# Expert biases carried by the weight loads and a product in plain fp32, and one attention chunk's output work regrouped, in an attention and mixture-of-experts kernel

## The chip, the cores and the metric

The kernel runs on one core of a Trainium2 chip. The metric is the time of one execution on the device in microseconds. The kernel before takes 384.93 us (median of 3 runs, 384.72 to 385.65).

## The reference

Input x is 2048 tokens of 128 numbers, all fp32. Two residual layers follow each other:

```
x = x + attn(layernorm(x))      # 16 heads of 64, linear attention with cos/sin weights,
                                # causal; (num / den) @ Wo + bo
x = x + ffn(layernorm(x))
ffn: logits = xf @ gate_w                       # 8 experts
     top_w, top_idx = top_k(logits, 2); top_w = softmax(top_w)
     h = gelu(xf @ w1[e] + b1[e])               # 128 -> 512
     y = h @ w2[e] + b2[e]                      # 512 -> 128
     out = sum over the two chosen e of y * top_w
```

The biases b1 and b2 are not zero here.

## The kernel before, in words

Tokens are cut into 16 chunks of 128, and four chunks make a unit; there are four units (NS). A unit has a front (projections of q, k and v as products of fp32 numbers split into a high and a low part, on the tensor engine) and then attention over its 16 groups of four heads, taken two at a time as pairs p. Each engine has its program written out by hand in one order; semaphores hold one engine for another. In a unit of the first three, the tensor engine does at the end of a pair: p = 3 and 5, `turn_out` of chunks 0 and 1 (eight transposes, L1238); p = 6, `project` of chunks 0 and 1 (32 instructions of L1247) and `turn_x` (the next unit's input, L1092); p = 7, `turn_out` of chunk 2; p = 8, `project` of chunk 2. Chunk 3 is turned and projected in the next front. The vector engine adds the projections to x (`residual`, L806).

While unit i is in its front and attention, the second layernorm, the gate and the routing of unit i-1 run beside it. The gate (`gate`) is `split3`: three products with split inputs for each chunk. The vector engine picks the two best experts, and GpSimd scatters every token's row, 128 numbers, its id and its weight, to its place in a DRAM buffer ybuf (L480), where every expert has its stretch. The output bias b2 is added per token: the vector engine builds a 128 x 8 matrix of weights for each chunk (`combine`), the tensor engine turns it (`turn_comb`, L1267), the scalar engine copies it, the tensor engine multiplies it by b2 (`biases`, L1273) and the vector engine adds the result (`open_sum`, L948). This is done for units 0 and 1 in the fronts of units 2 and 3, and for units 2 and 3 among the expert blocks.

The expert stage is 39 blocks (NB) of 128 rows of one expert. A small table, made in two parts (17 blocks, then 22), holds each block's expert and place. `block_table` makes it with products, four of which (L1302) fetch b1 for each block. SyncE's queue loads a block in `load_block`:

```
if b >= YR: sp.wait_ge(z_out[(b - YR) % ZR], ...)
at = sp.value_load(tab[0:1, 1, b:b + 1], ...)                  # L379
sp.dma_start(yb[b % YR][:], ybuf[bass.ds(at, TB), :])          # L380, the rows
if b >= WR: sp.wait_ge(h_ps, 2 * (b - WR) + 2)
sp.dma_start(w1b[b % WR][:], w1[bass.ds(at // PITCH, 1), ...]) # L383, the weights
```

YR = 10 row buffers, ZR = 8 result buffers and WR = 6 weight buffers go round. All of w2 stays in SBUF. A `step(b)` of the tensor engine is: transpose block b+2's rows (L1376), `hidden(b+1)` (eight instructions of L1389), `down(b)` (eight of L1404, into one PSUM bank). `down(b)` waits until the vector engine has taken block b-1's result. `weighed` (L1020) takes it: result times the row's weight, from PSUM into z. GpSimd scatters z to DRAM (L518); the results come back at the end (zin) and are added to x (L1027, L1029) and stored.

Of the kernel before, what the change touches and what calls it, by code (L numbers as in the profile page):

```python
# [28 lines left out]
P = 128  # L29
# [7 lines left out]
SC = 4  # L37
# [21 lines left out]
COMB_AT, BIAS_AT, BIAS_AFTER = 7, 9, 4  # L59
# [3 lines left out]
STATS_AFTER, NORM_AFTER, NORMED_AFTER, YLOW_AFTER, BEST_AFTER = 1, 2, 3, 5, 6  # L63
# [28 lines left out]
def moe_block(nc, x, Wq, bq, Wk, bk, Wv, bv, Wo, bo, gate_w, w1, b1, w2, b2,  # L92
              c_rot, c_pair, c_ident, c_small, c_tri, c_ids, out, ybuf, zbuf):
    with ExitStack() as ctx:
# [13 lines left out]
        gate_hi = sb("gate_hi", [P, E], F32R)  # L108
        gate_lo = sb("gate_lo", [P, E], F32R)
        brows = sb("brows", [2 * NP, P])  # L110
        bcols = sb("bcols", [P, 2 * NP])
        b1q = sb("b1q", [QC, F])
        bv_all = sb("bv_all", [P, HD])
        bo_all = sb("bo_all", [P, D])
        b2_sb = sb("b2_sb", [P, D])
# [25 lines left out]
        oT = sb("oT", [P, 2, NP, P])  # L141
# [6 lines left out]
        yT_hi = sb("yT_hi", [P, ST], F32R)  # L148
        yT_lo = sb("yT_lo", [P, ST], F32R)
# [9 lines left out]
        hotw = sb("hotw", [P, 2, SC, E])  # L159
# [11 lines left out]
        b1t = sb("b1t", [P, FB, NB])  # L171
        tab = sb("tab", [1, 2, NB], I32)
        comb = sb("comb", [P, SC, E])
        combT = sb("combT", [P, SC, P])
        yb = [sb(f"yb{k}", [P, ROW]) for k in range(3)]
        w1b = [sb(f"w1b{k}", [P, F]) for k in range(2)]
# [21 lines left out]
        w1b += [sb(f"w1b{k}", [P, F]) for k in range(2, WR)]  # L198
# [12 lines left out]
        b1_in = sem("b1_in")  # L211
# [58 lines left out]
        yThi_ok = sem("yThi_ok")  # L270
        yTlo_ok = sem("yTlo_ok")
# [9 lines left out]
        hotw_ok = sem("hotw_ok")  # L281
        any_ok = sem("any_ok")
        comb_ok = sem("comb_ok")
        cT_ps = sem("cT_ps")
        cT_ok = sem("cT_ok")
        b2_ps = sem("b2_ps")
        acc0_ok = sem("acc0_ok")
# [32 lines left out]
        def _(sp):  # L320
# [14 lines left out]
            sp.wait_ge(memsets, 2)  # L335
            sp.dma_start(b2_sb[0:E, :], b2).then_inc(c_in, 16)
# [15 lines left out]
            sp.wait_ge(memsets, 6)  # L352
# [10 lines left out]
            for e in range(E):  # L363
                sp.dma_start(b1q[e * QC // E:(e + 1) * QC // E, :], b1[e:e + 1, :].broadcast_to([QC // E, F])
                             ).then_inc(b1_in, 16)
# [47 lines left out]
        def _(pool):  # L413
            pool.memset(neg_half[:], -0.5).then_inc(memsets, 1)
            pool.memset(b2_sb[:], 0.0).then_inc(memsets, 1)
            pool.memset(combT[:], 0.0).then_inc(memsets, 1)
# [11 lines left out]
            pool.wait_ge(memsets, 5)  # L428
# [61 lines left out]
            def attention(i):  # L490
# [3 lines left out]
                for c in range(SC):  # L494
# [4 lines left out]
                    if c == 0:  # L499
                        if i == 0:  # L500
                            pool.wait_ge(c_in, 16 * 4)
# [37 lines left out]
        def _(act):  # L539
# [13 lines left out]
            act.wait_ge(row_in, 16 * 3)  # L553
            act.activation(gate_hi[:], gate_sb[:], ACT.Copy).then_inc(whi_ok, 1)
            act.wait_ge(bT_ok, 1)

            def turn_out(i, c):

                for half in range(2):
                    act.wait_ge(oT_ps, i * 2 * SC + 2 * c + half + 1)  # L560
                    act.activation(oT[:, c % 2, half * 4:half * 4 + 4, :],
                                   ps[:, 6 + half, :].rearrange("p (a b) -> p a b", b=P), ACT.Copy
                                   ).then_inc(oT_ok, 1)

            def front(i, tail):
# [5 lines left out]
                for j in range(QK_JOBS):  # L571
# [11 lines left out]
                    if i >= 2 and j == COMB_AT:  # L583
                        comb_turned(i - 2)
                keys(K_JOBS - 1)

            def y_turned(u, bank):
                n = len(UNITS[u][1]) * P
                act.wait_ge(yT_ps, u + 1)
                act.activation(yT_hi[:, 0:n], ps[:, bank, 0:n], ACT.Copy).then_inc(yThi_ok, 1)  # L590
# [9 lines left out]

            def comb_turned(i):
                act.wait_ge(cT_ps, i + 1)
                if i >= 1:
                    act.wait_ge(b2_ps, i)
                act.wait_ge(memsets, 4)
                act.activation(combT[0:E, :, :], ps[0:E, 7, :].rearrange("p (a b) -> p a b", b=P), ACT.Copy).then_inc(cT_ok, 1)
# [38 lines left out]
            def hidden(b):  # L645
# [7 lines left out]
                for f in range(FB):  # L653
                    if f % 2 == 0:
                        act.wait_ge(h_ps, b * 2 + f // 2 + 1)
                    act.activation(hT[:, b % 2, f, :], ps[:, b % 2 * 2 + f // 2, f % 2 * P:f % 2 * P + P], ACT.Gelu,  # L656
                                   bias=b1t[:, f, b:b + 1]).then_inc(h_ok, 1)
# [13 lines left out]
            for b in range(5, NB):  # L671
                hidden(b)
                if b == 10:
                    comb_turned(NS - 2)
                if b == 12:
                    comb_turned(NS - 1)
# [10 lines left out]
        def _(dve):  # L687
# [54 lines left out]
            def front(i, tail):  # L742
                angles(i)
                ones_columns(i)
                for m in range(V_JOBS):
                    if m == V_JOBS - 1:
                        if not tail:
                            dve.wait_ge(c_in, 16 * 4)
# [4 lines left out]
                    if not tail and m == 0:  # L753
                        low_half(0, 3)
                        dve.wait_ge(whi_ok, 4)
                        dve.tensor_tensor(gate_lo[:], gate_sb[:], f32(gate_hi[:]), ALU.subtract).then_inc(wlo_ok, 1)
# [6 lines left out]
                    if i >= 2 and m == BIAS_AFTER:  # L763
                        open_sum(i - 2)
                    if tail and m == YLOW_AFTER:
                        y_low(i - 1)
# [72 lines left out]
            def y_low(u, bank=6):  # L839
                n = len(UNITS[u][1]) * P  # L840
                dve.wait_ge(yThi_ok, u + 1)
                dve.tensor_tensor(yT_lo[:, 0:n], ps[:, bank, 0:n], f32(yT_hi[:, 0:n]), ALU.subtract).then_inc(yTlo_ok, 1)

# [35 lines left out]

            def combine(i):  # L880

                dve.wait_ge(wts_ok, i + 1 if i < NS - 1 else NU)
                if i >= 1:
                    dve.wait_ge(cT_ps, i)
# [625 lines left out]
```

## Time and profile before

| what | value |
|---|---|
| median of the runs shown | 384.93 us |
| the profiled execution: time | 386.15 us |
| the profiled execution: first to last instruction (span) | 384.3 us |
| tensor engine busy (of the span) | 353.2 us (92%) |
| vector, scalar, GpSimd busy | 61%, 41%, 34% |
| mean granted clock of the tensor engine | 0.98 |
| share of the chain that ended last: tensor engine, DMA, vector engine | 79%, 6%, 6% |

The profiled execution's own time is 1.85 us above its span and 1.22 us above the median. SPq is SyncE's instruction queue; its DMA rows are the time of the issue alone, and the transfer runs after it.

### The profile page before, as it was taken

The numbers are of one execution on the slowest core, as the hardware profiler recorded it, in microseconds if no ns is written. First come the engines' busy times: TensorE is split into PE (matmuls) and PEld (weight loads), VectorE is DVE, ScalarE is ACT, GpSimd is POOL, SyncE is SP. The second block draws the span as 40 slices with busy tenths as digits, with TensorE's granted clock in tenths as the row PEclk, the third lists the DMA queues.
The fourth block names the chain that finished last, engine by engine and source line by source line (L and its number), as shares of the span: only waits on it lengthen the run. The fifth ranks groups of instructions, "written<-read, shape, count | busy, mean of one in ns | idle before, by whom it ended". The sixth has DMA issues, their size and how long they took to land.

```text
span 384.3 us, 10812 instructions
## 1 busy us (share of the span) xinstructions
PE 353.2 (92%) x4167; PEld 320.9 (83%) x4167; DVE 236.3 (61%) x677; ACT 158.9 (41%) x374; POOL 130.4 (34%) x132
## 2 busy tenths in 40 slices
PE   0899999999999999999999999999999999999910
PEld 0677999988899988889999888999799999999910
DVE  4689864668886466797646678875646433222205
ACT  2575232267323136732322673122245455666600
POOL 5013241103058310304840130352326755555520
PEclk9999999999999999999999999999999999999975
DMA  7741332334001000000100001700463557877439
GB/s 250 197 185 63 147 143 107 131 124 159 2 31 33 25 9 3 0 2 26 40 25 9 2 0 31 206 25 20 115 172 109 163 142 211 231 200 205 124 83 244
DMA packets 32753, 38.35 MB, mean 100 GB/s; under 512 B 4115, under 2 KB 25008, under 8 KB 31680
## 3 DMA queue, kind: packets, MB, share of 16 engines
q1 hardware_dynamic: 27232, 31.62, 27.2%
q0 software_dynamic: 2272, 4.46, 3.3%
q10 hardware_dynamic: 3200, 1.58, 1.6%
q8 instruction: 34, 0.56, 0.6%
q14 instruction: 15, 0.12, 0.1%
HBM read 22.63 MB, written 15.47 MB: 99 GB/s over the span
## 4 chain that ended last, share of the span: by engine, by line
PE 79%; DMA 6%; DVE 6%; issue 3%; POOL 3%; SPq 1%; ACTq 0%; ACT 0%; POOLq 0%; DVEq 0%
PE ps L1211 8%; PE ps L1173 8%; PE ps L1404 7%; PE ps L1389 7%; PE ps L1190 7%; PE ps L1218 7%; PE ps L1247 7%; PE ps L1085 6%; PE ps L1087 6%; PE ps L1086 6%; PE ps L1238 4%; PE ps L1130 3%; DMA zin<-zbuf 2%; DMA yb<-ybuf 2%; POOL ybuf L480 2%
## 5 line engine op out<-in xcount | busy, mean ns | idle before, releaser
L615 ACT ACTIVATE os<-ps 128x260 f32<-128x260 f32 x64 | 24.8, 388 | 100.5 <-PE ps L1218 100.5
L656 ACT ACTIVATE hT<-ps,b1t 128x128 f32<-128x128 f32 x156 | 44.5, 368 | 34.8 <-PE ps L1389 34.0
L480 POOL DMA_INDIRECT ybuf<-yr,slot x32 | 31.7, 991 | 72.8 <-issue 37.4
L438 POOL TENSOR_TENSOR on<-tcs,rden 128x1024 f32<-128x1024 f32 x16 | 30.4, 1901 | 64.8 <-DVE rden L801 64.8
L518 POOL DMA_INDIRECT zbuf<-z,yb x39 | 37.9, 972 | 30.3 <-DVE z L1020 26.3
L788 DVE TENSOR_TENSOR state<-ps,state 128x260 f32<-128x260 f32 x64 | 27.4, 428 | 31.4 <-ACT os L615 29.1
L778 DVE TENSOR_TENSOR am<-ps,pair 128x1024 f32<-128x1024 f32 x32 | 38.7, 1210 | 9.9 <-issue 6.6
L1020 DVE TENSOR_SCALAR z<-ps,yb 128x128 f32<-128x128 f32 x39 | 13.7, 351 | 47.2 <-PE ps L1404 47.2
L1404 PE MATMUL ps<-w_sb,hT 128*128 x312 | 41.7, 277 | 0.8 <-DVE z L1020 0.8
L1211 PE MATMUL ps<-vcs,am 128*64 128x65 f32 x1024 | 42.2, 225 | 0.0
L1389 PE MATMUL ps<-xb,w1b 128*128 128x128 f32 x312 | 41.2, 276 | 0.0
L1211 PEld LDWEIGHTS ps<-vcs,am 128*64 128x64 f32 x1024 | 36.8, 137 | 3.9
L1218 PE MATMUL ps<-vcs,kn 128*64 128x130 f32 x512 | 39.5, 275 | 0.0
L1404 PEld LDWEIGHTS ps<-w_sb,hT 128*128 128x128 f32 x312 | 38.0, 192 | 1.4 <-issue 1.2
L1389 PEld LDWEIGHTS ps<-xb,w1b 128*128 128x128 f32 x312 | 38.1, 193 | 0.0
L1173 PE MATMUL ps<-qT,kT 64*128 64x128 f32 x512 | 37.2, 285 | 0.9 <-DVE am L778 0.9
L1173 PEld LDWEIGHTS ps<-qT,kT 64*128 64x128 f32 x512 | 31.1, 188 | 6.7 <-issue 6.2
L733 DVE TENSOR_TENSOR os<-ps,bv_all 128x512 f32<-128x512 f32 x32 | 22.1, 690 | 18.2 <-PE ps L1087 18.2
L1190 PE MATMUL ps<-state,qT 64*128 64x130 f32 x480 | 33.2, 277 | 0.0
L1247 PE MATMUL ps<-wo_sb,oT 128*128 128x128 f32 x256 | 31.6, 279 | 0.0
L737 DVE TENSOR_SCALAR vcs<-os,cs 128x512 f32<-128x512 f32 x64 | 30.9, 525 | 1.1
L1247 PEld LDWEIGHTS ps<-wo_sb,oT 128*128 128x128 f32 x256 | 29.8, 192 | 1.7 <-issue 1.4
(136 smaller groups left out, 619.6 us busy)
## 6 DMA issues: line engine op xcount, KB each, us to landing
w1b<-in_L_ffn_w SPq DMA_DIRECT2D x39, 256.0 KB, 3.1
ybuf<-blank SPq DMA_DIRECT2D x8, 1152.0 KB, 4.6
yb<-ybuf SPq DMA_DIRECT2D x39, 72.0 KB, 3.0
w_sb<-in_L_ffn_w SPq DMA_DIRECT2D x8, 256.0 KB, 4.6
x_sb<-in_L_attn_x SPq DMA_DIRECT2D x4, 256.0 KB, 5.2
pair<-c_pair SPq DMA_DIRECT2D x16, 64.0 KB, 2.0
zin<-zbuf SPq DMA_DIRECT2D x4, 256.0 KB, 5.6
zin<-zbuf ACTq DMA_DIRECT2D x4, 256.0 KB, 6.1
```

Source lines behind the costliest of these rows:

```text
L480: pool.indirect_dma_start(ybuf, bass.IndirectOffsetOnAxis(ap=slot[:, k, c:c + 1], axis=0), yr[:, k, c, :], None).then_inc(y_out[u], 16)
L518: pool.indirect_dma_start(zbuf, bass.IndirectOffsetOnAxis(ap=yb[b % YR][:, D:D + 1].bitcast(U32), axis=0), z[:, b % ZR, :], None, bounds_c ...
L656: act.activation(hT[:, b % 2, f, :], ps[:, b % 2 * 2 + f // 2, f % 2 * P:f % 2 * P + P], ACT.Gelu, bias=b1t[:, f, b:b + 1]).then_inc(h_ok, 1)
L737: last = dve.tensor_scalar(vcs[:, m // 2, (m % 2) * 8:(m % 2) * 8 + 8, s, 0:DH], vb[:, m % 2, :].rearrange("p (h d) -> p h d", d=DH), cs4[ ...
L778: dve.tensor_tensor(am[:, p % 2, :, :, :], ps[:, 0:2, :].rearrange("p r (q t) -> p r q t", t=P), pair[:, c, None, None, :].broadcast_to([P ...
L1173: last = mm(ps[:, r, b * P:(b + 1) * P], kT[rows, of, c * P:(c + 1) * P], qT[rows, of, c * P:(c + 1) * P], start=True, stop=True)
L1190: mm(ps[:, 2 + 2 * (n % 2) + r, 0:2 * CS].rearrange("p (s b v) -> p b s v", s=2, b=2)[:, q, :, :], qT[rows, 2 * g + q, c * P:(c + 1) * P], ...
L1211: mm(ps[t:t + 64, 2 + 2 * (n % 2) + r, q * VW:q * VW + VW], am[:, n // 2 % 2, r, (2 * g + q) % (PH // 2), t:t + 64], vcs[:, c, g * GH + 2 ...
L1218: last = mm(ps[64 * r:64 * r + 64, 2 + 2 * (n % 2) + q, 2 * CS:3 * CS], kn[:, c, (2 * g + q) * P + r * DH:(2 * g + q) * P + (r + 1) * DH], ...
L1247: last = mm(ps[:, 7, at:at + D], oT[:, c % 2, pr, :], wo_sb[:, pr, :], start=(pr == 0), stop=(pr == NP - 1))
L1389: last = mm(ps[:, b % 2 * 2 + f // 2, f % 2 * P:f % 2 * P + P], w1b[b % WR][:, f * P:(f + 1) * P], xb[:, b % XR, :], start=True, stop=True ...
L1404: last = mm(ps[:, 4, 0:D], hT[:, b % 2, f, :], w, start=(f == 0), stop=(f == FB - 1))
```

## The change

Six edits are made at once.

1. b1 is laid behind w1 on the host, so that a row of an expert's weights has 516 numbers in place of 512; the gelu takes its bias from there. The b1 loads, the four products of each table and the copy of b1t go away.
2. b2 comes by a third DMA in every `load_block`, one row of 128 numbers spread to 128 partitions, into six buffers b2b. `weighed` is two instructions: result plus b2b into zs, then zs times the weight into z. The matrix, its transposes, the bias products and `open_sum` go away for all four units.
3. `down` waits for zs (zs_ok), and the weight load of block b waits for zs of block b-6, in place of the hidden products of block b-6.
4. The gate is one plain fp32 product per chunk in place of three split ones; the vector engine's y_low goes away.
5. In the first three units, pair 6 has no projections; pair 7 has `third_chunk`: half of chunk 2's transposes, the projections of chunks 0 and 1, the other half; both halves use PSUM bank 6. Chunk 2 is projected in the next front after block 1. oT has three buffers.
6. The residual of chunks 0 and 1 stands after pair 7's groups on the vector engine.

```diff
+    columns = b.reshape(E, FB, P).transpose(0, 2, 1)
+    return np.ascontiguousarray(np.concatenate([w, columns], axis=2))
...
                 if b >= WR:
-                    sp.wait_ge(h_ps, 2 * (b - WR) + 2)
+                    sp.wait_ge(zs_ok, b - WR + 1)
                 sp.dma_start(w1b[b % WR][:], w1[bass.ds(at // PITCH, 1), :, :].rearrange("e p n -> p (e n)")
+                             ).then_inc(w1_in[b % WR], 16)
+                sp.dma_start(b2b[:, b % WR, :], b2[bass.ds(at // PITCH, 1), :].broadcast_to([P, D])
                              ).then_inc(w1_in[b % WR], 16)
...
                 dve.wait_ge(z_ps, b + 1)
+                dve.tensor_tensor(zs[:, b % 2, :], ps[:, 4, 0:D], b2b[:, b % WR, :], ALU.add).then_inc(zs_ok, 1)
                 if b >= ZR:
                     dve.wait_ge(z_out[b % ZR], 16 * (b // ZR))
-                dve.tensor_scalar(z[:, b % ZR, :], ps[:, 4, 0:D], yb[b % YR][:, D + 1:D + 2], None, ALU.mult
+                dve.wait_ge(zs_ok, b + 1)
+                dve.tensor_scalar(z[:, b % ZR, :], zs[:, b % 2, :], yb[b % YR][:, D + 1:D + 2], None, ALU.mult
...
-                if b == 10:
-                    open_sum(NS - 2)
-                    combine(NS - 1)
-                if b == 12:
-                    open_sum(NS - 1)
...
-                    if i >= 2 and j == COMB_AT:
-                        pe.wait_ge(x2_ok, i * SC)
-                        turn_comb(i - 2)
-                    if i >= 2 and j == BIAS_AT:
-                        biases(i - 2)
...
+            def third_chunk(i):
+                pe.wait_ge(on_ok, i * SC + 3)
+                turn_half(i, 2, 0, 6)
+                pe.wait_ge(oT_ok, i * 2 * SC + 4)
+                project(i, 0)
+                project(i, 1)
+                pe.wait_ge(oT_ok, i * 2 * SC + 5)
+                turn_half(i, 2, 1, 6)
...
-                    last = split3(ps[:, bank, c * E:(c + 1) * E], (yT_hi, yT_lo), (gate_hi, gate_lo),
-                                  lambda t: t[:, c * P:(c + 1) * P], lambda t: t[:])
+                    last = mm(ps[:, bank, c * E:(c + 1) * E], yT[:, c * P:(c + 1) * P], gate_sb[:], start=True, stop=True,
+                              skip_group_check=True)
...
-                for f in range(FB):
-                    mm(ps[:, bank, 352 + f * n:352 + (f + 1) * n], b1q[:, f * P:(f + 1) * P], match[:, 0:n],
-                       start=True, stop=True, skip_group_check=True)
...
-                    pe.wait_ge(z_ok, b)
+                    pe.wait_ge(zs_ok, b)
```

SyncE's queue, one block of the expert stage. Before (L379 reads the table, yb are the rows, w1b the weights):

```order
L379 TENSOR_LOAD tab
L379 ISA x2
L380 ISA
L380 DMA yb<-ybuf 128x144
L383 ISA
L383 DMA w1b<-in_L_ffn_w 128x512
```

The same block in the changed kernel, where b2b is the spread row of b2:

```order
L359 TENSOR_LOAD tab
L359 ISA x2
L360 ISA
L360 DMA yb<-ybuf 128x144
L363 ISA
L363 DMA w1b<-in_L_ffn_w 128x516
L365 ISA
L365 DMA b2b<-in_L_ffn_b 128x128
```

A register instruction and a DMA are added to each of the 39 blocks, between a block's weights and the next block's rows.

The tensor engine at the end of the first unit's attention, before, from the last groups of pair 6 (L1211, L1218: products of one group; L1173: scores; L1190: products with the state):

```order
L1218 MATMUL ps<-vcs,kn 64x130 x4
L1247 MATMUL ps<-wo_sb,oT 128x128 x16
L1092 MATMUL ps<-ident,xh 128x128 x4
L1173 MATMUL ps<-qT,kT 128x128 x8
L1190 MATMUL ps<-state,qT 128x2x65 x8
L1211 MATMUL ps<-vcs,am 64x65 x8
L1218 MATMUL ps<-vcs,kn 64x130 x4
L1211 MATMUL ps<-vcs,am 64x65 x8
L1218 MATMUL ps<-vcs,kn 64x130 x4
L1238 MATMUL ps<-ident,on 128x128 x8
L1190 MATMUL ps<-state,qT 128x2x65 x8
```

In the changed kernel, the same place:

```order
L1142 MATMUL ps<-vcs,kn 64x130 x4
L1021 MATMUL ps<-ident,xh 128x128 x4
L1097 MATMUL ps<-qT,kT 128x128 x8
L1114 MATMUL ps<-state,qT 128x2x65 x8
L1135 MATMUL ps<-vcs,am 64x65 x8
L1142 MATMUL ps<-vcs,kn 64x130 x4
L1135 MATMUL ps<-vcs,am 64x65 x8
L1142 MATMUL ps<-vcs,kn 64x130 x4
L1158 MATMUL ps<-ident,on 128x128 x4
L1185 MATMUL ps<-wo_sb,oT 128x128 x16
L1158 MATMUL ps<-ident,on 128x128 x4
L1114 MATMUL ps<-state,qT 128x2x65 x8
```

The 16 products stand between two halves of the transposes; `turn_x` stays where it is, behind pair 6.

The vector engine in the expert stage, before (xb is a turned block of rows):

```order
L1013 COPY xb<-ps 128x128
L1020 TENSOR_SCALAR z<-ps,yb 128x128
L1013 COPY xb<-ps 128x128
L1020 TENSOR_SCALAR z<-ps,yb 128x128
L1013 COPY xb<-ps 128x128
```

and in the changed kernel:

```order
L948 COPY xb<-ps 128x128
L953 TENSOR_TENSOR zs<-ps,b2b 128x128
L957 TENSOR_SCALAR z<-zs,yb 128x128
L948 COPY xb<-ps 128x128
L953 TENSOR_TENSOR zs<-ps,b2b 128x128
L957 TENSOR_SCALAR z<-zs,yb 128x128
```

Each block's result passes through two instructions, and only the first reads PSUM.

## Rows read from the trace of the kernel before

**Rows 1.** The page, busy time of each engine

```profile
PE 353.2 (92%) x4167; PEld 320.9 (83%) x4167; DVE 236.3 (61%) x677; ACT 158.9 (41%) x374; POOL 130.4 (34%) x132
```

**Rows 2.** Waits of the tensor engine: us, times, longest

```profile
PE ps L1313 <- DMA yb<-ybuf: 0.6, 1, 0.6
PE ps L1376 <- DMA yb<-ybuf: 0.3, 1, 0.3
```

**Rows 3.** Tensor engine in order of time, third front: start us, us

```profile
153.33 0.60 PE L1267 MATMUL ps<-ident,comb 128*8 128x128 f32 x4
153.76 0.60 PE L1130 MATMUL ps<-ident,kT 128*128 128x128 f32 x4
...
164.96 0.24 PE L1085 MATMUL ps<-gate_hi,yT_hi 128*128 128x8 f32 x1
165.06 0.25 PE L1086 MATMUL ps<-gate_lo,yT_hi 128*128 128x8 f32 x1
```

**Rows 4.** Chain of waits, expert stage, the bias product: start us, us

```profile
317.29 0.89 PE ps L1273 x8
```

**Rows 5.** Tensor engine, last unit, first block table

```profile
263.93 1.07 PE L1302 MATMUL ps<-match,b1q 128*128 128x17 f32 x8
264.93 0.20 PE L1304 MATMUL ps<-match,small 128*1 128x17 f32 x2
```

**Rows 6.** Tensor engine, end of the first unit, next front

```profile
61.61 3.84 PE L1247 MATMUL ps<-wo_sb,oT 128*128 128x128 f32 x32
65.28 0.60 PE L1092 MATMUL ps<-ident,xh 128*128 128x128 f32 x4
...
73.87 2.05 PE L1247 MATMUL ps<-wo_sb,oT 128*128 128x128 f32 x16
75.68 0.48 PE L1085 MATMUL ps<-xT_hi,W 128*128 128x512 f32 x1
```

**Rows 7.** Load queue (SPq) in order of time, expert stage

```profile
274.13 0.34 SPq L380 DMA_DIRECT2D yb<-ybuf  x1
...
316.56 0.34 SPq L380 DMA_DIRECT2D yb<-ybuf  x1
...
318.36 0.33 SPq L380 DMA_DIRECT2D yb<-ybuf  x1
318.92 0.33 SPq L383 DMA_DIRECT2D w1b<-in_L_ffn_w  x1
320.03 0.33 SPq L380 DMA_DIRECT2D yb<-ybuf  x1
...
336.00 1.33 SPq L383 DMA_DIRECT2D w1b<-in_L_ffn_w  x1
...
356.22 0.33 SPq L380 DMA_DIRECT2D yb<-ybuf  x1
```

**Rows 8.** Waits of the load queue, 308 to 360 us

```profile
SPq L379 <- DMA zbuf<-z,yb: 6.6, 3, 4.0
```

**Rows 9.** Page, DMA issues: KB each, median us to landing

```profile
yb<-ybuf SPq DMA_DIRECT2D x39, 72.0 KB, 3.0
```

**Rows 10.** Chain of waits, expert blocks and the end

```profile
321.98 0.11 PE ps L1376
...
361.79 0.11 PE ps L1376
...
365.51 0.36 DVE z L1020
```

**Rows 11.** Windows: busy us per engine (instructions), clock, DMA share, GB/s

```profile
104.00:108.00 4.00, 4.00 (x84) 3.70 (x82) 3.34 (x12) 0.87 (x3) 0.00 (x0) 1.00 0.06 16
344.00:350.00 6.00, 6.00 (x56) 6.00 (x55) 1.64 (x6) 3.73 (x15) 3.22 (x4) 1.00 0.77 221
```

**Rows 12.** Vector engine beside GpSimd, start of the second front

```profile
76.17 1.63 DVE L1001 COPY cnt<-small 128x8 f32<-128x8 f32 x1
```

**Rows 13.** GpSimd in the same stretch

```profile
75.87 1.91 POOL L438 TENSOR_TENSOR on<-tcs,rden 128x1024 f32<-128x1024 f32 x1 [10.36 <-DVE rden L801]
```

More of the change, by code:

```diff
@@ L170, in moe_block @@
         match = sb("match", [QC, NB])
-        b1t = sb("b1t", [P, FB, NB])
         tab = sb("tab", [1, 2, NB], I32)
-        comb = sb("comb", [P, SC, E])
-        combT = sb("combT", [P, SC, P])
         yb = [sb(f"yb{k}", [P, ROW]) for k in range(3)]
-        w1b = [sb(f"w1b{k}", [P, F]) for k in range(2)]
+        w1b = [sb(f"w1b{k}", [P, F + FB]) for k in range(2)]
+        b2b = sb("b2b", [P, WR, D])
+        zs = sb("zs", [P, 2, D])
         xb = sb("xb", [P, XR, P])
@@ L197, in moe_block @@
         w2_sb = sb("w2_sb", [P, E, F])
-        w1b += [sb(f"w1b{k}", [P, F]) for k in range(2, WR)]
+        w1b += [sb(f"w1b{k}", [P, F + FB]) for k in range(2, WR)]
         zin = sb("zin", [P, 2, NC, D])
@@ L656, in hidden @@
                     act.activation(hT[:, b % 2, f, :], ps[:, b % 2 * 2 + f // 2, f % 2 * P:f % 2 * P + P], ACT.Gelu,
[L657 removed]
+                                   bias=w1b[b % WR][:, F + f:F + f + 1]).then_inc(h_ok, 1)
             y_turned(NS - 1, 7)
@@ L964, in attention @@
                             residual(i, p // 2 - 2)
-                        elif p == 7:
-                            residual(i, 0, 2)
                     if tail and p == 1:
@@ L986, in attention @@
                         x_low(i + 1)
+                    if p == PAIRS - 1 and i + 1 < NS:
+                        residual(i, 0, 2)
             norm1_stats(0)
@@ L1142, in front @@
                         turn_out(i - 1, SC - 1)
+                    if tail and j == 1:
+                        project(i - 1, SC - 2)
                     if tail and j == WO_AT:
@@ L1229, in outputs, with turn_half @@
                     within(i, n, opening)
+            def turn_half(i, c, half, bank):
+                for q in range(4):
+                    pr = half * 4 + q
+                    last = pe.transpose(ps[:, bank, q * P:(q + 1) * P],
+                                        on[:, c % 2, 2 * pr:2 * pr + 2, :].rearrange("p h d -> p (h d)"), ident[:])
+                last.then_inc(oT_ps, 1)
             def turn_out(i, c):
                 pe.wait_ge(on_ok, i * SC + c + 1)
-                for half in range(2):
-                    if half == 1 and c >= (1 if i == NS - 1 else 2):
-                        pe.wait_ge(x2_ok, i * SC + c)
-                    for q in range(4):
-                        pr = half * 4 + q
-                        last = pe.transpose(ps[:, 6 + half, q * P:(q + 1) * P],
-                                            on[:, c % 2, 2 * pr:2 * pr + 2, :].rearrange("p h d -> p (h d)"),
-                                            ident[:])
-                    last.then_inc(oT_ps, 1)
+                turn_half(i, c, 0, 6)
+                if c >= (1 if i == NS - 1 else 3):
+                    pe.wait_ge(x2_ok, i * SC + c)
+                turn_half(i, c, 1, 7)
+            def third_chunk(i):
[6 more added lines that the diff above has]
+                turn_half(i, 2, 1, 6)
             def project(i, c):
@@ L1245, in project @@
                 at = D if c == 1 and i < NS - 1 else 0
+                if c == 2 and i < NS - 1:
+                    pe.wait_ge(x2_ok, i * SC + 2)
                 for pr in range(NP):
-                    last = mm(ps[:, 7, at:at + D], oT[:, c % 2, pr, :], wo_sb[:, pr, :], start=(pr == 0), stop=(pr == NP - 1))
+                    last = mm(ps[:, 7, at:at + D], oT[:, c % 3, pr, :], wo_sb[:, pr, :], start=(pr == 0), stop=(pr == NP - 1))
                 last.then_inc(wo_ps, 1)
@@ L1336, in attention @@
                             pe.wait_ge(xTlo_ok, i + 2)
-                        turn_out(i, p // 2 - 1)
+                        if p == PAIRS - 1 and i + 1 < NS:
+                            third_chunk(i)
+                        else:
+                            turn_out(i, p // 2 - 1)
                     if p % 2 == 0 and p >= 4:
@@ L1440, in _ @@
             step(9)
-            turn_comb(NS - 2)
-            step(10)
-            biases(NS - 2)
-            step(11)
-            pe.wait_ge(acc0_ok, NS - 1)
-            turn_comb(NS - 1)
-            step(12)
-            biases(NS - 1)
-            for b in range(13, NB):
+            for b in range(10, NB):
                 step(b)
 _INS = ["L0_attn_x", "L0_attn_Wq", "L0_attn_bq", "L0_attn_Wk", "L0_attn_bk", "L0_attn_Wv", "L0_attn_bv",
-        "L0_attn_Wo", "L0_attn_bo", "L0_ffn_gate_w", "L0_ffn_w1", "L0_ffn_b1", "L0_ffn_w2", "L0_ffn_b2"]
+        "L0_attn_Wo", "L0_attn_bo", "L0_ffn_gate_w", "L0_ffn_w1", "L0_ffn_w2", "L0_ffn_b2"]
 def shape_constants():
```

119 lines of the change are left out of this document (21 added, 98 removed).

## The prediction

> **What bounds the kernel now.** I read the page first: the tensor engine is busy 92% of the span, the others far less [rows 1]. Its waits are the second view, and they are nearly nothing once it has started: 0.6 us for the rows of expert block 1 and 0.3 us for a block's rows later on [rows 2]. So instructions taken off this engine shorten the kernel one for one, as long as nothing that it waits for is late. The third view is therefore the one that an engine's busy share does not show: the load queue, which issues each expert block's DMAs. In it the reader is to see the rhythm, not the waits. With no wait in between, a block's rows are issued at 318.36 and the next block's at 320.03, 1.66 us later, of which the second DMA with its register work is 318.92 - 318.36 = 0.56 us [rows 7]. The tensor engine takes one block in (361.79 - 321.98) / 21 = 1.896 us [rows 10]. The queue is thus 88% full in this stage before anything is added, and with its long issues (one of 1.33 us is shown) it needs (356.22 - 318.36) / 21 = 1.80 us a block [rows 7], 95% of the tensor engine's time.
>
> **The change part by part.** Times are of the profiled execution, 386.15 us with a span of 384.3; its 1.85 us outside the span I leave as they are. It lies 1.22 us above the median of the runs, 384.93, and a difference worked out in it is added to the median.
>
> *Bias products in the fronts.* In the fronts of units 2 and 3 go four transposes, 153.76 - 153.33 = 0.43 us [rows 3], and eight product instructions, 0.89 us [rows 4]. The tensor engine is full there, so 2 x 1.32 = 2.6 us come off.
>
> *Gate.* A unit's gate is twelve instructions, 0.10 to 0.11 us from start to start [rows 3]. A plain fp32 product of 128 x 128 weights runs as two instructions, as the eight of L1302 for four products show, at 1.00 / 8 = 0.125 us or less each [rows 5]. So four chunks take eight: 12 x 0.11 - 8 x 0.11 = 0.44 us less, by the dearer row 0.3. Three fronts: 1.3 us (0.9 to 1.3). The two gates of the last unit give 0.2 each, where the engine meets later waits; I count them as nothing.
>
> *Block tables.* The first loses eight instructions, 264.93 - 263.93 = 1.0 us in the last unit's attention [rows 5]. The second's are among the expert blocks, treated below.
>
> *Third chunk.* The same transposes and products are issued as before, in another place. What two stops cost is in two rows: 32 product instructions behind an attention group take 65.28 - 61.61 = 3.67 us, 0.115 each; sixteen take 75.68 - 73.87 = 1.81 us, 0.113 each [rows 6]. Against 0.111 inside a run [rows 4], entering from a group costs 0.1 us or less. And pair 6 keeps a stop, since the input's transposes stay there, as the order shows. I take 0 (from -0.3 for three units to +0.6, should chunk 2's rows or the residual arrive late). The residual of chunk 2 now holds the vector engine until the next front's second block. What is queued behind it is the copy of the angles and the values, for which the tensor engine waits at the next value product. That costs nothing, because the vector engine loses this time already: its first copy there took 1.63 us [rows 12], while GpSimd multiplied from 75.87 to 77.78 [rows 13], and now it starts when GpSimd is done. The Trainium skill, page SBUF — State Buffer, section Who interferes with whom, states that a vector instruction in its two-port mode and a GpSimd instruction shut each other out; the trace agrees in this copy.
>
> Before the expert stage that makes -(2.6 + 1.3 + 1.0) = -4.9 us.
>
> *First rows.* Block 1's rows were issued at 274.13 [rows 7] and the tensor engine already waited for them [rows 2]. A third DMA of block 0 now stands ahead, 0.56 us: +0.6.
>
> *Load queue.* The spread row of b2 adds the same pair to each block that the weights have, a register instruction and a DMA. Its price has bounds: 0 if the issue were hidden, 0.33 us for the bare issue, 0.56 with the register work and the gaps [rows 7]. I take 0.56, since the rows of one block stand end to end in this queue. A block then needs 1.66 + 0.56 = 2.22 us against 1.896 on the tensor engine: the queue becomes the bound. There is no store of loaded blocks to live on, because rows for blocks 10 to 16 wait for results scattered to DRAM (6.6 us of waits) [rows 8]. Block 16's rows are issued at 316.56; I take 315.8 in the changed kernel, as the second table and its b1 products are 1 us shorter ahead of those results. From there are 22 blocks to the last: 22 x 2.22 = 48.8 us. The long issues come on top: before, 356.22 - 316.56 - 22 x 1.66 = 3.1 us in 22 blocks [rows 7]. I keep 3.1 (1.5 if they go by the queue's load, 4.7 by the number of DMAs). The last block's rows are issued at 315.8 + 48.8 + 3.1 = 367.7 us. They land 3.0 us later [rows 9], at 370.7, where the tensor engine turned them at 361.79 before [rows 10]: +8.9 us. All the work that the change takes off the tensor engine among the expert blocks (bias products of two units, the second b1 products, the small gates, about 4 us) is lost in the waits for rows.
>
> The later release of weight buffers (zs of block b-6) costs nothing: when a step starts as its rows land, the end of step b-6 lies some 3.6 us ahead of the issue for block b. The DMA engines have room: a load of 64 KB in 512 byte rows occupied them for 0.06 x 4 = 0.24 us, and the share of 0.77 at 1.8 us a block [rows 11] becomes (1.39 + 0.24) / 2.3 = 0.71.
>
> *Tail.* The last result passes two instructions. The one of before took 0.36 us [rows 10]; I take +0.3 (0.2 to 0.4, and 1 us if GpSimd's scatter holds the second, which reads SBUF alone).
>
> Sum: -4.9 + 0.6 + 8.9 + 0.3 = +4.9 us. The long issues and block 16's start together move it by -2.2 and +2.4. I forecast 384.93 + 4.9 = 389.8 us; the case's own range is 387.6 to 392.2.
>
> The rule that speaks against this: the Trainium skill, page DMA: Bandwidth & Descriptors, section Issuing engines are not separate DMA queues, says that the sequencer's time to start a DMA is usually small beside the DMA itself. The issue is 0.33 us against 3.0 to landing, so the trace agrees for one DMA; but the landings overlap and the issues do not. By the rule the third load would be free, which is the first rival.
>
> **The rivals.**
>
> *The queue keeps up (not slower).* The place is the load queue, and it decides at a price of the third DMA under 1.896 - 1.80 = 0.1 us a block. For it: 95% was enough before, and the bytes are few. Against it: the issues stand end to end without waits. The time: -4.9 before the stage, +0.6, +0.3; among the blocks the queue's start after the scatters holds the engine, so that only the last bias product (0.9 us) is gained: -4.9 us, 380.0 us.
>
> *A thin third DMA.* Should it cost the bare issue, 0.33 us, and the long issues be 1.5 us, the last rows are issued at 315.8 + 22 x 1.99 + 1.5 = 361.1 and land at 364.1, +2.3 us: in all -4.9 + 0.6 + 2.3 + 0.3 = -1.7 to, with the long issues kept, -0.1 us. 384.0 us stands for it.
>
> *The queue and the DMA engines together.* If loads land later because 128 more packets a block share the engines with the scatters, result waits come back on the queue. At 2.5 us a block, 0.28 more than the queue's own pace, it is 22 x 0.28 = 6 us more: 395.8 us. The share of 0.77 speaks for it, the 0.24 us against it.
>
> *The regrouping fails in attention.* Three units in which pair 7 waits a microsecond for the normalised chunk: +3 us, 392.8 us. Against it: pairs 3 and 5 have the same distance from their groups to the transposes, and pair 7 has the input's transposes ahead besides.
>
> **How the numbers follow.** Forecast 0.73; queue keeps up 0.09; thin third DMA 0.08; both together 0.05; attention 0.05. The measurement tells about 0.3% from no change, 1.2 us. Faster by more than that (below 383.8): the first rival and part of the second, 0.12. Within: the rest of the second and the forecast's lowest edge, 0.06. Slower: 0.82. The range 384.0 to 393.2 us leaves the first rival and most of the third outside, with some of the forecast's upper edge, about 0.2.
>
> **What would show it.** In the changed profile the load queue should issue rows every 2.2 us from about block 14 on with hardly a wait, and the tensor engine should wait for yb in most of the last 24 blocks, some 0.4 us each, its busy share in that stage near 80%. The start of the expert stage should lie about 4.9 us earlier than before, and the tensor engine should have no new wait at pair 7 and none in the fronts. The forecast is wrong if the tensor engine's blocks still follow each other at 1.9 us, or if rows are issued earlier than the engine needs them; then the price of the third DMA was the failed step.

## The result and the profile after

| | median | runs | profiled execution | its span |
|---|---|---|---|---|
| before | 384.93 us | 384.72 to 385.65 | 386.15 us | 384.3 us |
| changed | 392.67 us | 391.14 to 393.69 | 391.79 us | 390.0 us |

The ratio is 1.0201, 95% interval 1.0164 to 1.0238: slower by 2%, or 7.7 us, where 389.8 us was forecast (range 384.0 to 393.2; the case's own range, 387.6 to 392.2, is missed by 0.5 us). A fourth execution of the kernel before took 914.58 us and is left out.

The page's first line answers to [rows 1]: the tensor engine has 4.5 us less to do, and yet the span grew by 5.7.

```profile
PE 348.7 (89%) x4087; PEld 314.0 (81%) x4087; DVE 235.3 (60%) x696; ACT 156.9 (40%) x369; POOL 129.9 (33%) x130
```

What it waits for, answering to [rows 2] (us, times, longest): the rows of the expert blocks, 9.3 us where it was 0.3. L1298 is the turning of a block's rows, L1235 that of blocks 0 and 1. The 0.7 us of L1158 is the last chunk's, at 278.92 (0.4 before); at pair 7 and in the fronts there is no new wait.

```profile
PE ps L1298 <- DMA yb<-ybuf: 9.3, 13, 1.4
PE ps L1235 <- DMA yb<-ybuf: 1.0, 1, 1.0
PE ps L1326 <- DVE zs L953: 0.7, 2, 0.5
PE ps L1158 <- POOL on L418: 0.7, 1, 0.7
```

The load queue in order of time (start, us), answering to [rows 7]. Nothing is waited for between these rows. The first two DMAs of a block stand 0.56 us apart as before, the third 0.52 behind the second, and the next block's rows 1.10 behind that: 2.18 us in place of 1.66. The later rows are a long issue and the rows of block 16 and of the last block.

```profile
301.68 1.25 SPq L365 DMA_DIRECT2D b2b<-in_L_ffn_b  x1
...
312.42 0.33 SPq L360 DMA_DIRECT2D yb<-ybuf  x1
...
335.68 0.33 SPq L360 DMA_DIRECT2D yb<-ybuf  x1
336.24 0.33 SPq L363 DMA_DIRECT2D w1b<-in_L_ffn_w  x1
336.76 0.33 SPq L365 DMA_DIRECT2D b2b<-in_L_ffn_b  x1
337.86 0.33 SPq L360 DMA_DIRECT2D yb<-ybuf  x1
...
363.57 0.33 SPq L360 DMA_DIRECT2D yb<-ybuf  x1
```

Its waits between 280 and 370 us, answering to [rows 8]. The last ends with block 13's rows, at 305.67; from there the queue only issues. The 3.3 us are block 6's weights, held until block 0's zs (edit 3). The queue then still waits 2.4 us for block 0's results before block 10's rows, so this wait costs nothing, as the prediction had it.

```profile
SPq L359 <- DMA zbuf<-z,yb: 4.4, 2, 2.4
SPq L363 <- DVE zs L953: 3.3, 1, 3.3
```

The chain that ended last, answering to [rows 10]. Before, it ran through the tensor engine's blocks one after the other; now rows from DRAM stand in it, and the last block's are issued at 363.57 and turned as they land:

```profile
342.37 3.90 DMA yb<-ybuf
346.64 0.90 PE ps L1311 x8
...
356.55 1.38 SPq L363
363.57 3.13 DMA yb<-ybuf
366.71 0.04 issue
366.75 0.33 PE ps L1298
...
370.74 0.30 DVE zs L953
...
372.76 0.49 DVE z L957
...
374.01 2.11 DMA zbuf<-z,yb
```

Windows of the changed kernel, as in [rows 11]. The engine is idle 4.4, 5.0 and 2.4 us in the three (the last is part of the first), at full clock, with the DMA engines at 0.75 to 0.81:

```profile
330.00:368.00 38.00, 33.59 (x282) 32.07 (x282) 13.29 (x49) 18.62 (x66) 15.52 (x16) 1.00 0.75 195
300.00:330.00 30.00, 25.01 (x203) 23.19 (x202) 9.79 (x36) 13.69 (x48) 15.56 (x17) 1.00 0.81 201
330.00:350.00 20.00, 17.64 (x150) 16.93 (x150) 6.79 (x25) 9.95 (x36) 7.76 (x8) 1.00 0.78 205
```

Ahead of the blocks all went as the change says. The third front's gate (answering to [rows 3]) and block 0 and 1's rows at the end of the attention:

```profile
162.83 0.95 PE L1198 MATMUL ps<-gate_sb,yT 128*128 128x8 f32 x8
163.64 0.41 PE L1059 MATMUL ps<-ident,kT 128*128 128x128 f32 x2
...
270.08 0.33 PE L1235 MATMUL ps<-ident,yb 128*128 128x128 f32 x1 [0.25 <-ACT oT L539]
271.42 0.33 PE L1235 MATMUL ps<-ident,yb 128*128 128x128 f32 x1 [1.01 <-DMA yb<-ybuf]
```

The same two, and the last block's, before:

```profile
275.47 0.33 PE L1313 MATMUL ps<-ident,yb 128*128 128x128 f32 x1 [0.25 <-ACT oT L561]
276.37 0.33 PE L1313 MATMUL ps<-ident,yb 128*128 128x128 f32 x1 [0.57 <-DMA yb<-ybuf]
...
361.62 0.27 PE L1376 MATMUL ps<-ident,yb 128*128 128x128 f32 x1
```

So the changed kernel is 5.4 us ahead at block 0, 5.0 at block 1, and 5.1 behind at the last block: 10.1 us are lost among the blocks.

### The profile page after: what moved, and what is told of

Same layout as the page of the kernel before. It is cut to its first block, busy times and chain, and to the rows that moved or that the text cites. A ratio compares the mean times of both kernels' runs of the same rounds, so it can differ in the third digit from the quotient of the medians.

```text
span 390.0 us, 10763 instructions
## 1 busy us (share of the span) xinstructions
PE 348.7 (89%) x4087; PEld 314.0 (81%) x4087; DVE 235.3 (60%) x696; ACT 156.9 (40%) x369; POOL 129.9 (33%) x130
## 4 chain that ended last, share of the span: by engine, by line
PE 69%; DMA 8%; SPq 7%; DVE 7%; issue 5%; POOL 2%; ACT 0%; ACTq 0%; POOLq 0%; DVEq 0%
PE ps L1097 8%; PE ps L1135 8%; PE ps L1114 7%; PE ps L1142 7%; PE ps L1185 6%; PE ps L1014 6%; PE ps L1015 5%; PE ps L1016 5%; PE ps L1326 4%; PE ps L1158 4%; PE ps L1311 3%; DMA yb<-ybuf 3%; PE ps L1059 3%; SPq L359 2%; SPq L363 2%
## 5 line engine op out<-in xcount | busy, mean ns | idle before, releaser
L625 ACT ACTIVATE hT<-ps,w1b 128x128 f32<-128x128 f32 x156 | 44.5, 368 | 47.3 <-PE ps L1311 44.7
L1326 PE MATMUL ps<-w_sb,hT 128*128 x312 | 42.8, 281 | 0.7 <-DVE zs L953 0.7
L953 DVE TENSOR_TENSOR zs<-ps,b2b 128x128 f32<-128x128 f32 x39 | 11.4, 291 | 45.0 <-PE ps L1326 43.7
L702 DVE TENSOR_SCALAR vcs<-os,cs 128x512 f32<-128x512 f32 x64 | 32.6, 552 | 1.1
L1114 PEld LDWEIGHTS ps<-state,qT 64*128 64x128 f32 x480 | 30.2, 188 | 0.8 <-issue 0.7
```

The costliest lines, as they stand in the source:

```text
L702: last = dve.tensor_scalar(vcs[:, m // 2, (m % 2) * 8:(m % 2) * 8 + 8, s, 0:DH], vb[:, m % 2, :].rearrange("p (h d) -> p h d", d=DH), cs4[ ...
L1114: mm(ps[:, 2 + 2 * (n % 2) + r, 0:2 * CS].rearrange("p (s b v) -> p b s v", s=2, b=2)[:, q, :, :], qT[rows, 2 * g + q, c * P:(c + 1) * P], ...
L1326: last = mm(ps[:, 4, 0:D], hT[:, b % 2, f, :], w, start=(f == 0), stop=(f == FB - 1))
```

## The experiments

The theory: the load queue's own issue of a third DMA, about half a microsecond, makes it slower than the tensor engine. The rivals: the extra bytes, or the kind of load (one row spread to 128 partitions); the new arithmetic and waits; the regrouping in attention. Three sets of kernels shared a chip and the kernel before each: its median was 385.15 us beside the first four, 384.96 beside the next four, 385.16 beside the last three.

### The same bytes in two DMAs

b2 is laid behind w1 and b1 on the host, already spread, so that a row has 644 numbers.

```diff
-    return np.ascontiguousarray(np.concatenate([w, columns], axis=2))
+    rows = np.broadcast_to(b2[:, None, :], (E, P, D))
+    return np.ascontiguousarray(np.concatenate([w, columns, rows], axis=2))
...
-                sp.dma_start(b2b[:, b % WR, :], b2[bass.ds(at // PITCH, 1), :].broadcast_to([P, D])
-                             ).then_inc(w1_in[b % WR], 16)
```

> The changed kernel with b2's row laid behind w1 and b1 on the host (a row of 644 numbers), so that a block is two DMAs again; the bytes are those of the changed kernel. Theory (the third issue on the load queue is the price): the queue returns to 1.66 us a block, the tensor engine's waits for yb fall from 9.3 us to about 1, and the time is 379.5 us, 378 to 382. Rival (the 64 KB more a block on the DMA engines are the price): the bytes stay, so the waits stay and the time is at least 388 us. Rival (the second instruction of weighed and the later release of the weight buffers are the price): both stay too, 388 us or more.

Measured: 384.3 us (382.03 to 385.23, 10 runs), ratio 0.9968, interval 0.9947 to 0.9989. Against the changed kernel 8.4 us are back, from the same arithmetic and the same bytes; but not the 379.5 expected (378 to 382). Where the rest is, its tensor engine shows (waits, then windows of 2 us):

```profile
PE ps L1295 <- DMA yb<-ybuf: 2.9, 3, 1.4
...
PE ps L1232 <- DMA yb<-ybuf: 1.8, 1, 1.8
```

```profile
270.00:272.00 2.00, 0.57 (x3) 0.35 (x3) 0.14 (x1) 0.00 (x0) 0.00 (x0) 0.91 0.63 207
272.00:274.00 2.00, 2.00 (x17) 1.81 (x16) 0.28 (x1) 0.38 (x1) 0.00 (x0) 0.50 0.80 214
274.00:276.00 2.00, 2.00 (x44) 1.87 (x44) 0.00 (x0) 0.28 (x1) 0.00 (x0) 0.74 0.87 238
```

It waited 1.8 us for block 1's rows, in part since the issue of block 0's weights, ahead of them on the queue, took 1.12 us:

```profile
266.38 1.12 SPq L362 DMA_DIRECT2D w1b<-in_L_ffn_w  x1
268.29 0.33 SPq L359 DMA_DIRECT2D yb<-ybuf  x1
```

and then ran 3 us (272 to 275) at a granted clock of 0.50, the lower of its two levels (1.2 GHz).

### The same bytes in three DMAs

The row of 644 numbers is loaded in two pieces, of 516 and 128 numbers.

```diff
-                sp.dma_start(w1b[b % WR][:], w1[bass.ds(at // PITCH, 1), :, :]...
+                sp.dma_start(w1b[b % WR][:, 0:F + FB], w1[bass.ds(at // PITCH, 1), :, 0:F + FB]...
+                             ).then_inc(w1_in[b % WR], 16)
+                sp.dma_start(w1b[b % WR][:, F + FB:F + FB + D], w1[bass.ds(at // PITCH, 1), :, F + FB:F + FB + D]...
```

> The kernel of e1_merged with its weight load cut in two DMAs, 516 numbers a row and then 128, same bytes, same buffers. Theory (issue): a block's rows every 2.2 us again, 391 to 394 us, as the changed kernel. Rival (what cost was reading one row of b2 128 times): the source is 128 different rows here, so the time stays near e1_merged. Rival (bytes): no difference between e1_merged and this one.

Measured: 390.96 us (389.79 to 393.03, 6 runs), ratio 1.0152, interval 1.0127 to 1.0177; the expectation said 391 to 394. Its queue has the changed kernel's rhythm, 2.18 us from rows to rows, and its tensor engine the same wait:

```profile
337.65 0.33 SPq L359 DMA_DIRECT2D yb<-ybuf  x1
338.21 0.33 SPq L362 DMA_DIRECT2D w1b<-in_L_ffn_w  x1
338.73 0.33 SPq L364 DMA_DIRECT2D w1b<-in_L_ffn_w  x1
339.83 0.33 SPq L359 DMA_DIRECT2D yb<-ybuf  x1
```

```profile
PE ps L1298 <- DMA yb<-ybuf: 10.1, 12, 1.3
```

Of this pair only the number of DMAs differs (and with it that of their packets, at nearly the same busy share of the DMA engines, 29.2% against 29.0%), and 6.7 us lie between them. So the bytes are not what costs them. The spread source could be worth no more than the 1.7 us from here to the changed kernel, and the runs of the two overlap.

### The third DMA alone, in the kernel before

For blocks 8 to 38 it loads b2's row of the block's expert, spread to 128 partitions, into a free buffer; nothing reads it, but the tensor engine waits until it has landed.

```diff
+                if b >= 8:
+                    sp.dma_start(zin[:, 0, b % WR, :], b2[bass.ds(at // PITCH, 1), :].broadcast_to([P, D])
+                                 ).then_inc(d3_in[b % WR], 16)
...
+                if b >= 8:
+                    pe.wait_ge(d3_in[b % WR], 16 * ((b - 8) // WR + 1))
```

> The kernel before with nothing changed but a third DMA on the load queue for blocks 8 to 38: b2's row spread over 128 partitions into memory that nobody reads. Theory (issue): 31 blocks at 2.2 us from block 14 on; the last rows are issued near 368 us in place of 356.2, and the time is 393.5 us, 391.5 to 396. Rival (the delay comes from what the vector engine does with b2, or from the release of the weight buffers): neither is here, so 385 to 386 us.

Measured: 397.15 us (395.73 to 398.7), ratio 1.0312, interval 1.0285 to 1.0338: 12.0 us for a DMA whose data nobody uses (10.3 by the spans of the profiled executions), above the 391.5 to 396 expected. The last rows go out near the expected 368 us, but they are turned at 371.79, 10.2 us later than before, where the expectation adds 8.6 in all, and 2.8 us of the profiled execution lie outside its span in place of 1.85. Its rows are issued at 316.45 (block 16) and 368.74 (the last), 2.377 us a block, and the tensor engine waits:

```profile
PE ps L1380 <- DMA yb<-ybuf: 7.1, 7, 1.7
```

### The changed kernel without the regrouping

The two stops, the residual and the chunk's projections are put back as they were (edits 5 and 6 undone).

```diff
-                        if p == PAIRS - 1 and i + 1 < NS:
-                            third_chunk(i)
-                        else:
-                            turn_out(i, p // 2 - 1)
+                        turn_out(i, p // 2 - 1)
```

> The changed kernel with the regrouping of chunk 2 undone (pair 6 projects chunks 0 and 1 again, pair 8 chunk 2), biases and gate as changed. Theory (the regrouping is worth 0): the same as the changed kernel within 0.6 us, and the first rows of the expert stage turned at 270.1 to 270.7 us. Rival (the regrouping is what saved the 0.5 us more than forecast before the expert stage): the first rows turned at 270.6 us or later and the time up to 1.5 us longer. Rival (it costs): shorter than the changed kernel by over 1 us.

Measured: 392.9 us (391.47 to 395.71), ratio 1.0217, interval 1.0185 to 1.0249, against 392.67 with it: no difference that these runs, 2.5 and 4.2 us wide, can tell. Its first rows are turned at 269.50, earlier than the 270.1 to 270.7 expected; but the profiles with the regrouping have 269.34 to 270.37, so this does not decide either. Whether the queue hides something is asked again below.

### Block 1's rows ahead of the first weights

Blocks 0 and 1 are loaded as rows, rows, weights, weights, in three kernels: the changed one, the merged row, the kernel before.

```diff
-            load_block(0)
-            load_block(1)
+            for b in range(2):
+                ats.append(sp.value_load(tab[0:1, 1, b:b + 1], min_val=0, max_val=PLACES))
+                sp.dma_start(yb[b][:], ybuf[bass.ds(ats[b], TB), :]).then_inc(yb_in[b], 16)
+            for b in range(2):
+                sp.dma_start(w1b[b][:], w1[bass.ds(ats[b] // PITCH, 1), :, :].rearrange("e p n -> p (e n)")
...
```

> The changed kernel with the rows of blocks 0 and 1 issued before the weights and bias rows of either. Nothing else is moved. Theory (besides the third issue, the wait for block 1's rows, 1.0 us in the profile of the changed kernel, lets the granted clock of the tensor engine fall in some executions, which is why its runs lie between 391.1 and 393.7 us): the wait goes, the runs come together within 1 us, and the median is 390.8 us, 390 to 391.6. The long stretch after block 13 is bound by the load queue as before and gives back part of the gain. Rival (the spread comes from the long issues of the load queue): the median is the changed kernel's, 392 to 393.5, with the same spread.

Measured: 391.3 us (388.9 to 392.36, 6 runs), ratio 1.0153, interval 1.0124 to 1.0182. The median is as expected, 1.4 us under the changed kernel's; but the runs did not come together within 1 us, they lie 3.5 apart. The wait for block 1 is gone, and 8.4 us of waits for rows stay.

> The kernel of e1_merged (two DMAs a block) with the rows of blocks 0 and 1 issued first. In the profile of e1_merged the tensor engine waited 1.8 us for block 1's rows, and the granted clock was 0.50 from 272 to 274 us. Theory (that wait and the clock that fell behind it kept e1_merged from 379.5 us): 381 us, 380 to 382.3, no granted clock under 1.00 between 268 and 290 us. Rival (the clock falls for another reason, or the time was lost at blocks 13 to 15): 383.5 to 384.5 us.

Measured: 379.76 us (379.36 to 380.25, 5 runs), ratio 0.9864, interval 0.9845 to 0.9883. It is 4.5 us under the merged row alone (3.5 by the profiled executions) and just under the expected 380 to 382.3, though the wait removed was 1.8 us. The merged row's ten runs have mean granted clocks from 0.970 to 0.978, these five from 0.977 to 0.982. The clock stays up in the same stretch:

```profile
270.00:272.00 2.00, 2.00 (x36) 1.71 (x38) 0.43 (x1) 0.38 (x1) 0.00 (x0) 1.00 0.89 255
272.00:274.00 2.00, 2.00 (x41) 1.82 (x38) 0.88 (x3) 0.78 (x2) 0.00 (x0) 1.00 0.81 243
```

> The kernel before with the rows of blocks 0 and 1 issued first. It waited 0.6 us for block 1's rows, with the clock at 1.00. Theory: 0.3 to 0.8 us less than before, 384.6 us. Rival (an order of loads that only helps where the clock falls): no difference within 0.3 us.

Measured: 384.92 us (384.04 to 385.71, 12 runs), ratio 0.9992, interval 0.9979 to 1.0006: no difference, as the rival said, where 0.3 to 0.8 us were expected. The order of the first loads gave much, 4.5 us, in the one kernel where the profile shows the clock fall behind the wait.

### Twelve row buffers in place of ten

```diff
-YR, ZR, WR, XR = 10, 8, 6, 4
+YR, ZR, WR, XR = 12, 8, 6, 4
```

On the merged row with block 1's rows first:

> The kernel of e6 with 12 row buffers in place of 10, so that block b's rows wait for the results of block b-12 and not b-10. Theory (in e1_merged the last loss of time is that blocks 13 to 15 wait for results scattered late, 2.9 us of waits in all): 2 us less than e6, 379 us, 378 to 380.5. Rival (the queue's own 1.66 us a block leaves too small a lead, or the waits move to another block): within 0.7 us of e6.

Measured: 376.9 us (375.93 to 378.43, 6 runs), ratio 0.9792, interval 0.9766 to 0.9818. This is 2.9 us under ten buffers, where 2 were expected (378 to 380.5). It is the best of all versions, 2.1% faster than the kernel before. Its tensor engine hardly waits for rows, is full where the changed kernel's was not, and the queue waits again:

```profile
PE ps L1300 <- DMA yb<-ybuf: 0.4, 1, 0.4
```

```profile
300.00:330.00 30.00, 29.65 (x263) 29.28 (x262) 11.76 (x45) 17.71 (x63) 18.80 (x20) 1.00 0.85 244
330.00:350.00 20.00, 20.00 (x182) 20.00 (x181) 8.55 (x33) 11.72 (x42) 10.34 (x11) 1.00 0.86 241
```

```profile
SPq L362 <- DVE zs L955: 11.2, 13, 6.3
```

The same on the kernel before (also with rows first), as a control (the text says 8 row buffers where it means ten):

> The kernel before, with the rows of block 1 asked for ahead of the first weights and 12 row buffers in place of 8; still two DMAs a block. Theory: this kernel's stretch of the blocks was bound by the tensor engine, with about 1 us of waits for rows in it, so the buffers can give back only that: 384.5 us, between 383.5 and 385.5. Rival: the buffers alone are what the merged row with 12 buffers gained over the merged row with 8 (2.9 us), whatever the arithmetic: 382.

Measured: 384.55 us (383.87 to 384.89, 12 runs), ratio 0.9976, interval 0.9963 to 0.999. Two DMAs a block and a full tensor engine: the buffers give 0.4 us. The other 7.6 us of the version above (384.55 - 376.9) come from the change with its merged row.

On that version, with the regrouping undone:

> The merged row with block 1's rows first and 12 row buffers, and the projections of the chunks regrouped back as they were before the change. Theory: the regrouping is worth nothing: within 0.5 us of the same kernel with it (376.9). Rival: with the queue no longer the bound, what the regrouping gives or takes ahead of the blocks shows: 1 us or more to either side.

Measured: 377.2 us (376.18 to 377.93), ratio 0.9785, interval 0.9766 to 0.9805, against 376.9 with it. With hardly a wait for rows to hide it, the regrouping still gives and takes nothing that can be told: runs of one kernel lie 1.8 and 2.5 us apart here.

On the changed kernel with its three DMAs (and rows first):

> The changed kernel, three DMAs a block, with block 1's rows first and 12 row buffers. Theory: the load queue issues at its own 2.18 us a block, and buffers help it only where it waited for one to come free, ahead of the first long stretch of issues (about 2.4 us of such waits in the changed kernel); 388.8 us, between 387.5 and 391. Rival: the wait for rows comes from jitter of the issues that more buffers would even out, as they did for the merged row: 385 or less.

Measured: 386.82 us (385.27 to 388.44, 12 runs), ratio 1.0042, interval 1.0026 to 1.0059. It lies 0.7 us under the theory's range and 1.8 over the rival's. The part that the theory named came larger: block 16's rows are issued at 306.93, against 310.32 with ten buffers. And the pace from there was 2.254 us a block against 2.413, since in the profiled execution no long issue fell between (four did with ten buffers, the longest 1.44 us). Whether that is the buffers or chance, one profile of each does not tell. The queue stays the bound (5.8 us of waits for rows), and this kernel 9.9 us above the same with a merged row.

## Why the prediction was right, step by step

The mechanism forecast is the one found: the third load's issue makes the load queue the bound, and what comes off the tensor engine is given back in waits for rows. Two DMAs in place of three give 8.4 us back, and with block 1's rows first 11.5 (391.3 - 379.76); three pieces for the same bytes take 6.7 again.

- *Ahead of the expert stage*: forecast -4.9, measured 270.08 - 275.47 = -5.4. Most of the difference is in the gates: a unit's runs from 162.83 to 163.64, 0.81 us for eight instructions, against 1.34 for twelve, which is 0.53 each and 1.6 for three where 1.3 was taken. Other profiles with the same work ahead of the blocks turn the first rows at 269.34 to 270.37, so the last tenths say little.
- *Regrouping*: forecast 0, and no difference in two pairs of kernels (392.67 and 392.9; 376.9 and 377.2), which cannot tell some tenths of a microsecond. The rival in attention is out.
- *First rows*: forecast +0.6, measured 5.4 - 5.0 = +0.4.
- *Price of the third DMA*: taken as 0.56 us, measured 0.52 (2.18 - 1.66). Over 22 blocks that is 0.9 us too much, while what comes on top of that pace took 3.2 in place of 3.1: 51.9 us forecast, 363.57 - 312.42 = 51.15 measured. The prediction calls these 3.1 us long issues; here the one long issue, of 1.38 us, is 1.05 of the 3.2, and the rest are many delays of 0.1 to 0.4 us in issues and register reads. The thin third DMA and the queue that keeps up are out.
- *Block 16's start* is the step that missed. It was to be issued 0.8 us earlier than the first blocks' shift gives (316.56 - 5.0 = 311.6), and was issued at 312.42, 0.8 later: 1.6 us off. I had taken the results' return from the kernel before. What decides is block 13, whose rows wait for block 3's result to come back. Its scatter was issued 5.0 us earlier, like the rest, but took longer to land (before, then the changed kernel, from the two chains):

```profile
305.55 2.24 DMA zbuf<-z,yb
300.59 4.33 DMA zbuf<-z,yb
```

So block 13's rows went out at 305.67 against 308.53, 2.9 us earlier in place of 5.0. Behind them the changed kernel's queue ran at its own pace, where the one before waited 2.5 us more (the 6.6 us of [rows 8] are waits of blocks 13 to 16 alone, not of 10 to 16, as the prediction reads them). The long issue of 1.25 us at 301.68 is no part of it: behind it the queue still waited 2.0 us for that result. In the first five kernels of the experiments, which all load more a block than the kernel before, the same transfer took 2.92 to 3.78 us; why was not tested. That waits for results still hold this stretch, twelve buffers showed: block 16's rows went out 3.4 us earlier.
- *Landing*: 3.13 us against 3.0. The forecast set this against 361.79, where the engine before turned the last rows; that instruction starts at 361.62, 0.2 us more.
- *Both queues*: the forecast's 3.1 us of long issues held, the DMA share was 0.75 to 0.81 where 0.71 was forecast, but no wait for results came back after block 16, which that rival needs. The later landing ahead of block 13 is all of it that the trace shows.
- *Idle of the tensor engine*: forecast as some 0.4 us in most of the last 24 blocks and a busy share near 80%; the waits are 13, of 0.7 on average, and the share is 25.01 / 30 = 83% from 300 to 330 us and 33.59 / 38 = 88% from there. The waits are fewer and longer than a mean pace makes them.
- *Tail*: +0.3 forecast, +0.6 measured (the last scatter's transfer starts 374.01 - 368.31 = 5.7 later, the last rows were turned 5.1 later). The last result took 0.88 us from the start of its first instruction to the end of its second, where one instruction took 0.35, so +0.5, above the range of 0.2 to 0.4:

```profile
372.21 0.97 POOL L498 DMA_INDIRECT zbuf<-z,yb  x1 [0.83 <-DVE z L957]
372.36 0.29 DVE L953 TENSOR_TENSOR zs<-ps,b2b 128x128 f32<-128x128 f32 x1 [0.92 <-PE ps L1326]
372.76 0.47 DVE L957 TENSOR_SCALAR z<-zs,yb 128x128 f32<-128x128 f32 x1
```

Of the last 0.47 us GpSimd's scatter accounts for 0.18: with no scatter beside it the instruction takes 0.29. It took 0.30 a block earlier, at 371.14, and both times it ended 0.05 us behind the end of the scatter beside it (371.39 and 373.18). The Trainium skill, page SBUF — State Buffer, section Who interferes with whom, states that a vector instruction in its two-port mode and a GpSimd instruction shut each other out; the trace agrees here. It agrees too where it was used for the third chunk: the copy of 1.63 us [rows 12] now starts at 77.29, 0.2 us before GpSimd's product ends (the prediction had it start behind), takes 0.24, and ends with the product as before.

Together the profiled executions differ by 391.79 - 386.15 = 5.6 us, where 4.9 was forecast. That this is so near is in part luck: block 16's start made it 1.6 us longer, while the price of the third DMA (0.9 us too much) and the part ahead of the blocks (-5.4 and +0.4 in place of -4.9 and +0.6) made it shorter. The medians differ by 7.7. The profile before lay 1.2 us above its median and this one 0.9 below its own, and executions of one kernel spread by more than that: 23 of the kernel before from 383.85 to 386.5, four of the changed one from 391.14 to 393.69. So a forecast made between profiles was 0.7 us short, and the same forecast, added to a median, 2.9. With that the time lies outside the case's own range and inside the wider one put forward. Which step holds the other 2 us stays open: the kernel without the regrouping, at 392.9, says that the higher median is real. A queue that is the bound passes on whatever long issues and small delays it meets (beyond 2.18 us a block, its last 22 took 3.2 us more here, 5.1 with the rows first, 1.6 with twelve buffers), which would do it; that was not shown run by run. Nor is a clock lowered in some executions by the wait for block 1 excluded: the mean granted clock is 0.981 in the profiled execution and 0.975 to 0.978 in the other three, and 0.979 to 0.982 in the six with the rows first, 1.4 us faster by the median; but one of the three, at 0.977, is the fastest of the four.

The rule weighed in the prediction (the Trainium skill, page DMA: Bandwidth & Descriptors, section Issuing engines are not separate DMA queues: the time to start a DMA is usually small beside it) would have made the change faster. For one DMA the trace agrees again, 0.33 us against 3.1. But the merged and the split row differ by 6.7 us with the same bytes, so the third load is not free, and the measurement decides: in this stream the issues add up and the transfers overlap.

## What to carry to other kernels

Before a load is added to a stream, read the issuing queue's rhythm from start to start and set it against the consumer's time per step: no view of waits shows that 1.66 us of issue against 1.90 of work leave room for only half a DMA more. Where a small operand goes with a large one, lay both in one row on the host: in a DMA of their own the bytes of b2 cost some 7 us more than as part of the 322 KB DMA. And when a bound moves, ask again what the buffers are for: two more row buffers gave 0.4 us to the kernel before, 2.9 to the merged row and 4.5 to the changed kernel.

## What the runs showed of the hardware

- A wait of 1.8 us of the tensor engine was followed by 3 us at a granted clock of 0.50. Without the wait the profiled execution was 3.5 us shorter and the median 4.5, not 1.8. Waits of 0.6 and 1.0 us at the same place (the kernel before and the changed one) left the clock at 1.00, and so did one of 2.0 us among the blocks (the changed kernel without the regrouping, ending at 313.14): the length of a wait alone does not tell.
- Some issues on the load queue take 0.9 to 1.7 us in place of 0.33, one to four in a stage of 100 us, on any of a block's DMAs. What causes them was not found.
- A vector instruction of 0.29 us that reads and writes SBUF took 0.47 beside a scatter of GpSimd and ended 0.05 us behind it.
- Eight plain fp32 instructions for a product with 128 x 8 inputs take 0.10 us each, no more than each of the twelve split ones.
